# A second token shift built from two scaled copies of the norm instead of a difference and two multiply-adds

## What is computed

```
x = x + att * g @ Wo.T
xn2 = _ln(x, ln2_w, ln2_b)
sx2 = _token_shift(xn2, state[:, i0])      # previous token minus this one; for token 0 the given state row
xk = xn2 + sx2 * ffn_maa_k
xr = xn2 + sx2 * ffn_maa_r
rr = sigmoid(xr @ ffn_Wr.T)
kk = square(relu(xk @ ffn_Wk.T))
x = x + rr * (kk @ ffn_Wv.T)
```

## Time and profile before

| | before |
|---|---|
| median of 3 runs | 589.7 us (588.98 to 591.48) |
| the profiled execution | 592.12 us, span 590.3 us |
| mean granted TensorE clock | 0.921 of full speed |
| busy, of the span | DVE 489.1 us (83%), PE 459.1 (78%), PE weight loads 254.6 (43%), ACT 289.2 (49%), POOL 75.7 (13%) |
| moved by DMA | 69.33 MB |

### The profile page before, as it was taken

The page is one execution under the profiler, slowest core; times in us unless marked ns, Lnnn a source line. Parts: engine busy times, 40 slices in busy tenths (PEclk is TensorE's granted clock), DMA queues, the critical chain, the costliest instruction groups (busy, mean ns, idle before and its releaser), DMA issues.

```text
span 590.3 us, 5701 instructions
## 1 busy us (share of the span) xinstructions
PE 459.1 (78%) x1952; PEld 254.6 (43%) x1952; DVE 489.1 (83%) x502; ACT 289.2 (49%) x623; POOL 75.7 (13%) x91
## 2 busy tenths in 40 slices
PE   0767787978798879977998889878988797456434
PEld 0553543634364436532653355334634473243222
DVE  1349889879999999999899999997999899866221
ACT  4253563467435752784365646554545543422341
POOL 0100101210122022201310111210120102100000
PEclk9997987998899899998898999988989799959859
DMA  8070661794399129942895179614990693100200
GB/s 296 37 180 14 145 149 37 152 217 121 63 222 234 34 47 217 218 90 38 198 221 113 36 169 226 131 36 96 207 197 1 143 221 64 36 28 0 36 0 27
DMA packets 26693, 69.33 MB, mean 117 GB/s; under 512 B 1576, under 2 KB 19624, under 8 KB 24232
## 3 DMA queue, kind: packets, MB, share of 16 engines
q1 hardware_dynamic: 19416, 54.55, 37.8%
q0 software_dynamic: 7248, 14.42, 13.9%
HBM read 46.15 MB, written 12.19 MB: 99 GB/s over the span
## 4 chain that ended last, share of the span: by engine, by line
PE 42%; DVE 26%; issue 17%; DMA 7%; ACT 6%; POOL 1%; SPq 0%; DVEq 0%; POOLq 0%
PE pa L730 12%; PE pc L737 9%; DVE kv L438 8%; DVE x L365 4%; DMA vrep<-v_scratch 3%; DVE kv L428 3%; DVE kv L446 3%; PE pc L730 3%; PE pc L878 3%; PE patt L861 3%; DMA v_scratch<-v_sb 3%; PE pa L768 2%; PE pb L756 2%; PE pc L722 2%; PE pb L768 2%
## 5 line engine op out<-in xcount | busy, mean ns | idle before, releaser
L438 DVE TENSOR_TENSOR_SCAN kv<-w_sb,kv 128x512 f32<-128x512 f32 (+2 forms) x144 | 146.3, 1086 | 0.0
L730 PE MATMUL pa<-x,large_sb 128*128 128x512 f32 (+2 forms) x288 | 129.8, 598 | 1.6 <-ACT xn L583 1.4
L730 PEld LDWEIGHTS pa<-x,large_sb 128*128 128x128 f32 x288 | 59.8, 214 | 65.0 <-issue 58.5
L428 DVE TENSOR_TENSOR kv<-vrep,k_sb 128x2016 f32<-128x2016 f32 (+2 forms) x36 | 72.6, 2016 | 6.0 <-DMA vrep<-v_scratch 5.3
L446 DVE TENSOR_TENSOR kv<-kv,r_sb 128x2048 f32<-128x2048 f32 (+2 forms) x36 | 72.8, 2045 | 0.0
L321 POOL COPY kv<-s_sb 128x32 f32<-128x32 f32 (+2 forms) x36 | 24.3, 678 | 327.5 <-PE patt L861 327.5
L768 PE MATMUL pb<-th,w_sb 32*128 32x512 f32 (+2 forms) x108 | 39.0, 660 | 24.2 <-DVE x L365 24.2
L365 DVE SCALAR_TENSOR_TENSOR x<-pb,vec_sb,sx 128x512 f32<-128x512 f32 (+2 forms) x72 | 46.1, 683 | 9.1 <-PE pb L768 4.9
L861 PE MATMUL patt<-kv,const_sb 128*32 128x512 f32 (+2 forms) x288 | 36.0, 590 | 13.7 <-DVE kv L446 13.7
L878 PE MATMUL pc<-sq,const_sb 128*128 128x512 f32 (+2 forms) x36 | 22.3, 756 | 23.4 <-ACT sq L661 23.4
L737 PE MATMUL pc<-large_sb,xr 128*128 128x256 f32 x128 | 33.5, 420 | 7.9 <-DVE xr L492 7.9
(11 more groups left out here) (87 smaller groups left out, 730.9 us busy)
## 6 DMA issues: line engine op xcount, KB each, us to landing
vrep<-v_scratch SPq DMA_DIRECT2D x12, 2048.0 KB, 18.3
x<-xn POOLq DMA_DIRECT2D x18, 512.0 KB, 7.7
vrep<-v_scratch SPq DMA_DIRECT2D x4, 1536.0 KB, 10.8
x_tok<-in_x SPq DMA_DIRECT2D x6, 512.0 KB, 24.6
v_scratch<-v_sb SPq DMA_DIRECT2D x12, 256.0 KB
xres<-in_x SPq DMA_DIRECT2D x6, 512.0 KB, 22.4
out<-xres SPq DMA_DIRECT2D x6, 512.0 KB, 10.3
out<-trr POOLq DMA_DIRECT2D x6, 512.0 KB, 9.5
```

The source lines that it names most:

```text
L428: dve.tensor_tensor(kv[:, q % 2, :, 0:nb, 1:L], vv[:, G4 * j:G4 * (j + 1), :, 0:L - 1], kk, ALU.mult).then_inc(kv_ready, 1)
L438: ins = dve.tensor_tensor_scan(flat, w_sb[:, p, q % HF, 0:nb].rearrange("p b t -> p (b t)"), flat, 0.0, ALU.mult, ALU.add)
L730: ins = pe.matmul(dst[:, m, 0:n], w(a)[:, m * P:(m + 1) * P], src[:, a, 0:n], start=(a == 0), stop=(a == HF - 1))
```

## The change

It does three things.

1. The shift is rewritten. With m for `ffn_maa_r` or `ffn_maa_k`, xn2 + m * (previous - xn2) is previous * m + xn2 * (1 - m). Before the loop ACT makes per-feature vectors `past_w`, `past_b`, `now_w`, `now_b` of these factors times weight and bias of the norm (16 instructions of one element in each partition). In `xn2` ACT then reads the transposed norm in PSUM four times per half (eight instructions instead of two): `past_r` and `xr`, `past_k` and `xk`. DVE's `shift2` only adds `past` shifted by one token into `xr` and into `xk`, each as one instruction for token 0 and one for tokens 1 to 63. For the first chunk DVE also scales the state rows (`put_prev`, four small instructions). `RR` on PE now also waits until ACT has read all of `pc` (`now_k_ready`).
2. All five order tables are others.
3. Some small tiles are merged into one (`filled`, `stats1`, `stats2`), with no change in what is computed.

```diff
-DVE_ORDER = [("a3", 3), ("mix4", 2), ("sc2", 3), ("sc3", 3), ("rs2", 3), ("rs3", 3), ("rk", 2), ("out", 4),
...
+DVE_ORDER = [("mix4", 2), ("sc3", 3), ("rs2", 3), ("rs3", 3), ("rk", 2), ("out", 4), ("att", 3), ("a0", 2),
...
-PE_ORDER = [("P4", 2), ("W1", 1), ("X01", 1), ("WO", 3), ("S0", 2), ("X2", 1), ("P0", 1), ("X3", 1), ("S1", 2),
...
+PE_ORDER = [("M", 3), ("P4", 2), ("VR", 3), ("W1", 1), ("X01", 1), ("WO", 3), ("S0", 2), ("P0", 1), ("X2", 1),
+            ("X3", 1), ("T2", 3), ("S1", 2), ("P1", 1), ("X4", 1), ("RR", 3), ("D1", 1), ("KK", 3), ("D2", 1),
+            ("P3", 1), ("Y2", 3), ("S2", 2), ("S3", 2), ("T1", 0), ("CB", 1)]
...
+ACT_ORDER = [("w", 2), ("r", 2), ("xn", 1), ("sq", 3), ("tg", 2), ("rstd", 3), ("th", 1), ("st", 0),
+             ("st2", 3), ("nrm2", 3), ("v", 1), ("xn2", 3), ("k", 1), ("nrm", 0), ("rr", 3), ("thd", 1),
              ("kk", 3)]
...
-SP_ORDER = [("lx", 2), ("vst", 3), ("sx2", 5), ("vl0", 3), ("vl1", 3), ("lr", 4)]
...
+SP_ORDER = [("lr", 5), ("vst", 3), ("lx", 1), ("vl0", 3), ("sx2", 5), ("vl1", 3)]
...
             def c_shift(c, p):
-                dve.wait_ge(xn2_ready, c + 1)
+                if c == 0:
+                    put_prev()
+                    dve.wait_ge(prev_put, 2)
                 nb, n = extent(c)[0:2]
-                seqs = [ap[:, :, 0:n].rearrange("p a (b t) -> p a b t", t=L) for ap in (sx2, xn2)]
-                dve.tensor_tensor(seqs[0][:, :, :, 0], prev_sb[:, 0, :, FIRST[c]:FIRST[c] + nb], seqs[1][:, :, :, 0], ALU.subtract)
-                dve.tensor_tensor(seqs[0][:, :, :, 1:L], seqs[1][:, :, :, 0:L - 1], seqs[1][:, :, :, 1:L], ALU.subtract).then_inc(sx2_ready, 1)
-                dve.wait_ge(sx2_ready, c + 1)
-                for dst, name, done in ((xr, "ffn_r", xr_ready), (xk, "ffn_k", xk_ready)):
-                    for a in range(HF):
-                        ins = dve.scalar_tensor_tensor(out=dst[:, a, 0:n], in0=sx2[:, a, 0:n], scalar=vec(name, a),
-                                                       in1=xn2[:, a, 0:n], op0=ALU.mult, op1=ALU.add)
-                    ins.then_inc(done, 1)
+                for now, before, first, made, done in ((xr, past_r, prev_r, now_r_ready, xr_ready), (xk, past_k, prev_k, now_k_ready, xk_ready)):
+                    dve.wait_ge(made, c + 1)
+                    now, before = [ap[:, :, 0:n].rearrange("p a (b t) -> p a b t", t=L) for ap in (now, before)]
+                    dve.tensor_tensor(now[:, :, :, 0], now[:, :, :, 0], first[:, :, FIRST[c]:FIRST[c] + nb], ALU.add)
+                    dve.tensor_tensor(now[:, :, :, 1:L], now[:, :, :, 1:L], before[:, :, :, 0:L - 1], ALU.add).then_inc(done, 1)
...
             def c_xn(c, p):
                 act.wait_ge(t2_done, c + 1)
...
-                for a in range(HF):
-                    ins = act.activation(xn2[:, a, 0:n], pc[:, a, 0:n], ACT.Identity, bias=vec("ln2_b", a), scale=vec("ln2_w", a))
-                ins.then_inc(xn2_ready, 1)
...
+                for now, before, name, done in ((xr, past_r, "r", now_r_ready), (xk, past_k, "k", now_k_ready)):
+                    for a in range(HF):
+                        act.activation(before[:, a, 0:n], pc[:, a, 0:n], ACT.Identity, bias=shift_vec("past_b", name, a), scale=shift_vec("past_w", name, a))
+                        ins = act.activation(now[:, a, 0:n], pc[:, a, 0:n], ACT.Identity, bias=shift_vec("now_b", name, a), scale=shift_vec("now_w", name, a))
+                    ins.then_inc(done, 1)
...
             def rr(c, p):
+                pe.wait_ge(now_k_ready, c + 1)
                 pe.wait_ge(xr_ready, c + 1)
```

71 lines of the change are left out of this document (46 added, 25 removed).

## The result

The changed kernel takes 603.5 us (median of 4 runs, 603.02 to 604.13), the kernel before beside it 590.5 (588.98 to 591.48): a ratio of 1.024, 95% interval 1.020 to 1.027. Forecast were 586.2 us and a range up to 593. The change makes the kernel slower by 13 us, and the prediction had the sign wrong.

A forecast was written before the change was run, and what follows sets the result against it. DVE looked like the bound, PE close behind and taking over in the middle. Terms +0.7 - 3.0 - 2.3 + 0.7 - 3.0 - 0.8 + 4.2 = -3.5 us, against the median of 589.7, gave 586.2 us; range 579 to 593.

The forecast's parts named there:

- Part 1: DVE arithmetic: 1.5 us less per full chunk, 12 us in all, time only where DVE ends last.
- Part 2: ACT arithmetic: eight instructions, 5.8 us instead of 1.45, between T2 and RR; covered in the middle, not at the end.
- Just covered: Middle: ACT's 5.8 us after T2 fits behind PE's S1, P1 and X4, 6.2 us.
- the +35 us: Whole kernel: the loss if ACT were the bound, 8 x 4.4 us; left out of the sum.
- Part 3: Four middle iterations: PE becomes the bound, the long kind goes, a pause ahead of X3 may lower the clock; -3.0 us.
- the short iteration: Middle: the kind of about 60.2 us before the change, from 309.06 to 369.24; forecast to stay 60.0.
- Part 4: Start: 16 small ACT instructions cost 3.4 us, earlier P0 gains 1.8, mix4 gains 0.9; net +0.7.
- Part 5: Chunks 1 to 3: -3.0 and -2.3 us, put_prev +0.7; the iteration from 432.17, -0.8.
- Part 6: End: table load ahead of rstd +1.3, uncovered activations make +2.8 for chunk 7, +1.4 for chunk 8; together +4.2 us.
- (a): Middle and start: low clock in every iteration, no gain at the start; about -0.5 us, 589.2 us; chance 0.25.
- (b): Middle: DVE is the bound after all, PE's run from T2 compresses; iterations 58.7, time 577.8 us; chance 0.10.
- (c): Iterations: slower through DMA, vrep lands late and DVE waits before a0 and a1; 598 us; chance 0.12.

The follow-up runs named there:

- the mended tables: The changed kernel's order tables with P4 behind VR and tg behind rstd; with small instructions late, new sum 590.7 us; kernel before's arithmetic 591.6 us.
- the run on the two moves alone: The kernel before, own arithmetic and tables, but P0 ahead of X2 on PE and nrm2 ahead of v on ACT: 593.2 us.
- the kernel of 581.1 us: The changed kernel with P4 behind VR, tg behind rstd, small instructions in the first xn2, and three unread matmuls ahead of X3: 581.1 us.

## Why the prediction was wrong, by its own steps

**Part 1, DVE, was right in size.** The page has 11.0 us less work. What it is worth as time isn't one number: under the mended tables the old sum is 0.9 us from the new one, within what the runs can tell, under the changed kernel's own tables 5.8 us.

**Part 2, ACT, was right in size.** Eight activations follow at 0.66 to 0.67 us: 5.4 us where 5.8 was forecast. "Just covered" holds in the middle, in the changed kernel (ACT is done at 352.3, `RR` starts at 353.82) and with `P4` put back (346.5 and 348.04, when PE has done `X4`). Under the old tables they are not covered, and the arithmetic costs 17 us with its small instructions. The Trainium skill (ScalarE: Activation LUTs, Rules for kernel authors) speaks against such work on ScalarE; the +35 us that the prediction worked out for an ACT that is the bound, no run shows.

**Part 3, the middle, is the main step that failed.** The profiled pair differs by +11.2 us where the sum had -3.5. Of these 14.7 us, 6.5 lie in the four middle iterations and 1.5 in the one behind them; 5.9 lie at the start, 3.1 at the end, and chunks 1 to 3 have 2.3 the other way. For the middle the prediction laid the new lists on the short iteration from `X2` on: "DVE up to `rs1` is the same list, so `res` ends at 333.1". The lists differ ahead of that, on PE: `P4` stands ahead of `VR`. The prediction priced one pause, the one ahead of `X3`, and rightly: forecast 3.6 us, measured 3.47 with `P4` put back (2.73 in the changed kernel). It didn't look for the others, 1.89 and 2.06 us ahead of `X01` and `WO`. Those cost the clock of `WO`, 2.9 us, and by `res` and `nrm2` the time of `T2`. In the kernel with `P4` put back the rest of the part can be read off: `T2` 32.8 us behind `att` (forecast 32.5), `RR` at 41.8 (forecast 40.3 with the full clock, 41.4 with the low one), the iteration 61.4 (60.0 and 61.1). `X3`, `T2` and `S1` all run at half speed, 2.6 us, where it counted 1.7 for `T2` and `P1`, less 0.6 of slack. What it got wrong there is mostly the mixture: it took 60.8 us for the mean of the four, and the low clock came in each. The Trainium skill (TensorE: Matmul & The Clock Gate, HAM oscillation) says that idle stretches between bursts throttle the array again; the runs bear this out, and of the two ends the prediction should have taken that one.

**Part 4, the start.** The small instructions took 3.1 us on ACT (forecast 3.4). This is the second step that failed, by 5.9 us in the profiled pair (+6.6 for +0.7). The gains against them aren't seen: in the run on the two moves alone, with `P0` ahead of `X2`, the first `att` is at 75.5 us, not below the 73.4 of before. By medians, the 16 instructions cost 4 to 6 us. A single first `att` says little, though: with lists that are the same up to there it came at 74.3, 75.2 and 80.0 us.

**Part 5, chunks 1 to 3, had the sign, and its causes aren't shown.** The table has -6.9 us where -4.6 was forecast with `put_prev` in it. But the kernel before with 16 small instructions at the start, and its own tables, has -4.2 there too. Up to the third `att`, start and chunks together, the change has -0.3 us where the parts had -3.9. The iteration behind the middle, +0.7 for -0.8, shares the fault of part 3.

**Part 6, the end, had the sign and one of two mechanisms, too small:** +7.3 for +4.2. From `T2` to `RR` it is +1.2 in chunk 7 and +1.1 in chunk 8 (forecast for chunk 8: 1.4). In the rest the low clock shows: `WO` of chunk 7 takes 6.08 us (3.72 before), `WO` of chunk 8 5.49 (4.37), `RR` of chunk 8 4.78 (4.35 in the earlier trace rows). It isn't the place of `P4`, nor the table load ahead of `rstd`, to which the part gave 1.3 us: with both put back the end is only 0.4 us shorter, and with the old sum besides it is still 103.8 us, 5.3 more than before.

**The rivals.** (a), the low clock in every iteration and no gain at the start, was the mechanism in the middle, and its own sign came (a mean clock of 0.892, below 0.92); its price was the fault: 589 us, since it had the one pause only. (b) needs PE's run to be shorter; from `RR` to `att` it is 19.7 us even with the clock held. (c) had the sign and came nearest, with 598 us, by the wrong cause: `a0` and `a1` wait for no load in the middle. The trace of before gave what was needed: `WO` at 3.72 us behind a pause of 0.40, and `VR` at 3.63 us behind one of 2.40 in one iteration (at 1.98 and 1.99 behind the same pause in two others). Each move of work out of a place asks what PE does at that place afterwards, and that question was put for `X2` and `X3` only.

## What to carry to other kernels

When a list is reordered, go through every wait of the matrix unit in the new order, not only through those on the path, and write the length of the pause beside it; two pauses of 2 us in front of a long projection cost it 3 us more by the clock here. Matmuls that nobody reads, put into such pauses, part the clock's cost from that of the order and may be worth keeping, but they have to be sized from a row of their own shape: six in a pause gave +5 us, since they overran it, and three, which fitted, -10 us. Work taken off a full engine has no fixed worth: the same 11 us gave 6 us under one set of tables and 1 us or nothing under another.

## What the runs showed of the hardware

- **At the start the matmuls run at half speed while the granted clock reads 1.00,** and for how long differs between executions of the same lists. `P0`, `P1` and `X4` of the first chunk, in the changed kernel:

```profile
24.68 3.78 PE L759 MATMUL pa<-x,large_sb 128*128 128x256 f32 x8 [1.71 <-DVE x L378]
...
31.75 3.78 PE L759 MATMUL pa<-x,large_sb 128*128 128x256 f32 x8
35.32 3.52 PE L826 MATMUL pb<-th,w_sb 128*128 128x64 f32 x16
```

  and in the kernel with `P4` put back, the same up to there:

```profile
24.38 3.78 PE L759 MATMUL pa<-x,large_sb 128*128 128x256 f32 x8 [1.70 <-DVE x L378]
...
30.60 1.99 PE L759 MATMUL pa<-x,large_sb 128*128 128x256 f32 x8
32.43 1.89 PE L826 MATMUL pb<-th,w_sb 128*128 128x64 f32 x16
```

  with the granted clock (third number from the end) in this stretch, first of the one and then of the other:

```profile
20.00:45.00 25.00, 21.32 (x91) 16.04 (x84) 7.09 (x14) 8.62 (x27) 1.59 (x3) 1.00 0.46 108
...
20.00:45.00 25.00, 18.68 (x98) 13.82 (x98) 10.64 (x20) 12.35 (x32) 1.59 (x3) 1.00 0.48 111
```

  The first `att` came at 80.0 and 74.3 us, and at 75.2 in a third kernel that is the same up to there. The table of stretches above may therefore overstate the start. The Trainium skill (TensorE: Matmul & The Clock Gate, Seeing it yourself) warns that the records of the clock gate are not to be trusted one by one; these rows agree.
- **The same pause doesn't always cost the clock.** In the kernel of 581.1 us PE waits 2.42 us ahead of `VR` in one iteration and `VR` takes 1.98 us; in the next it waits 2.45 us and `VR` takes 3.40:

```profile
307.82 1.98 PE L916 MATMUL pc<-sq,const_sb 128*128 128x512 f32 x4 [2.42 <-ACT sq L673]
...
367.57 3.40 PE L916 MATMUL pc<-sq,const_sb 128*128 128x512 f32 x4 [2.45 <-ACT sq L673]
```

- **A 128x512 matmul of float32 has two records and takes 0.9 us** at the full clock (six in 5.42 us), twice what one record suggests.
- **An activation that reads PSUM follows the next at 0.66 to 0.67 us** for 128x512, although each is listed with 0.77 to 0.81 us, so eight take 5.4 us and not 6.2.
